# Four row buffers for the experts' gathers, beta added between scatters, and sixteen successive tokens per partition

## The reference, cut to what matters

```python
x = x + tanh(g_xattn[0]) * L0_xattn(layernorm(x), ctx)
x = x + tanh(g_ffn[0])   * L0_ffn(layernorm(x))      # shared expert + top-1 of 8, silu(gate) * up, down
x = x + tanh(g_xattn[1]) * L1_xattn(layernorm(x), ctx)
x = x + tanh(g_ffn[1])   * L1_ffn(layernorm(x))      # top-2 of 8, relu, down
# L1_ffn ends with
y = mixed + x_in                       # x_in: the layernormed rows; mixed: weighted sum of two experts
return gamma * (y - mu) * rsqrt(var + eps) + beta
```

## Time and profile before

| | |
|---|---|
| median of 3 runs | 1531.54 us (1530.1 to 1533.1) |
| the profiled execution | 1530.35 us |
| its span in the trace | 1528.6 us |
| PE busy | 1335.6 us, 87% of the span |
| ACT busy | 972.7 us, 64% |
| DVE busy | 561.1 us, 37% |
| POOL busy | 194.6 us, 13% |

### The profile page before, as it was taken

How to read it: one execution, slowest core, us unless ns; L and a number is a source line. 1 busy time by engine, 2 the same in 40 slices (tenths; PEclk the granted TensorE clock), 3 DMA queues, 4 the chain that set the end, 5 groups by cost and what they waited for, 6 DMA issues and landing times. The chain is left out here.

```text
span 1528.6 us, 31785 instructions
## 1 busy us (share of the span) xinstructions
PE 1335.6 (87%) x13156; PEld 699.0 (46%) x13156; DVE 561.1 (37%) x1257; ACT 972.7 (64%) x1146; POOL 194.6 (13%) x188
## 2 busy tenths in 40 slices
PE   6799999999999996999279999999999972799940
PEld 4433333333334555999233334334334332688840
DVE  7412142432333343333631223323323327333327
ACT  4499999999994323222159987987987930343322
POOL 2000000000001411332100000000000000644434
PEclk9899999999999997999679999999999985899975
DMA  7661001001114522111456100100101240121241
GB/s 206 158 113 30 23 23 27 18 18 28 26 29 151 179 78 87 49 49 39 103 160 111 27 18 16 42 17 16 41 17 50 87 136 27 49 63 63 66 141 55
DMA packets 76617, 100.80 MB, mean 66 GB/s; under 512 B 10074, under 2 KB 62302, under 8 KB 75704
## 3 DMA queue, kind: packets, MB, share of 16 engines
q1 hardware_dynamic: 70520, 82.47, 20.1%
q0 software_dynamic: 5952, 16.26, 3.3%
HBM read 67.99 MB, written 26.21 MB: 62 GB/s over the span
## 5 line engine op out<-in xcount | busy, mean ns | idle before, releaser
L1180 ACT ACTIVATE arena<-ps 128x1024 f32<-128x1024 f32 x556 | 557.5, 1247 | 56.4 <-PE ps L947 56.4
L947 PE MATMUL ps<-arena 99*32 99x512 bf16 x6656 | 463.9, 384 | 15.0 <-PEq L797 9.4
L947 PEld LDWEIGHTS ps<-arena 99*32 99x32 bf16 x6656 | 149.3, 95 | 408.5 <-issue 166.0
L1180 ACT ACTIVATE wqkv<-ps 128x1024 f32<-128x1024 f32 x276 | 298.2, 1248 | 22.7 <-PE ps L947 22.7
L963 PE MATMUL ps<-arena 128*32 128x512 f32 x2224 | 288.8, 594 | 0.8 <-ACT arena L1180 0.8
L1262 DVE COPY work<-ps 128x512 f32<-128x512 f32 x32 | 22.1, 691 | 404.6 <-PE ps L963 404.6
L1644 PEld LDWEIGHTS ps<-work,arena 128*128 128x128 f32 x1184 | 144.7, 195 | 6.5 <-DVE work L1723 3.5
L1644 PE MATMUL ps<-work,arena 128*128 128x128 f32 x1184 | 145.8, 279 | 2.1 <-DVE work L1723 2.1
L963 PE MATMUL ps<-wqkv,arena 128*32 128x512 f32 x1104 | 142.9, 593 | 0.0
L1822 POOL DMA_INDIRECT work<-xn_img,fetch x62 | 60.6, 977 | 630.5 <-POOLq L927 612.4
L1656 PE MATMUL ps<-arena,work 128*128 x496 | 119.3, 384 | 5.5 <-issue 5.0
(11 more groups left out here) (202 smaller groups left out, 1145.3 us busy)
## 6 DMA issues: line engine op xcount, KB each, us to landing
arena<-in_ew SPq DMA_DIRECT2D x16, 512.0 KB, 5.4
arena<-q_img SPq DMA_DIRECT2D x32, 192.0 KB
arena<-y_tok SPq DMA_DIRECT2D x12, 512.0 KB, 7.2
arena<-k_img SPq DMA_DIRECT2D x8, 624.0 KB, 12.7
q_img<-work SPq DMA_DIRECT2D x18, 256.0 KB, 2.6
k_img<-work SPq DMA_DIRECT2D x21, 208.0 KB, 2.5
arena<-q_img SPq DMA_DIRECT2D x32, 128.0 KB
work<-work SPq DMA_DIRECT2D x128, 32.0 KB, 2.0
```

Of the source, the lines that this page charges most:

```text
L947: last = nc.tensor.matmul(ps[i * VW:(i + 1) * VW, buf + j, :], k2[0:ROWS + SHIFT, h, at:at + VW], q2[0:ROWS + SHIFT, h, :], start=True, st ...
L1180: nc.scalar.activation(probs[(b * STEPS + u) % RING], ps[:, buf:buf + 2, :], ACT.Exp, scale=SCALE).then_inc(s_exp, 1)
```

## The change

Three edits, of which the third has several places:

1. `ROWBUFS` is 4: a fourth `rows_in` buffer, so that POOL gathers four tiles ahead of the one whose results it waits for.
2. In layer 1 `beta` is added in 16 instructions of 128 x 256, one behind each of the first 16 scatters, in place of four instructions of 128 x 1024 ahead of the loop.
3. Token `p*16 + t` is now `x[p, t, :]` (the view `(p t) d -> p t d`). A partition holds sixteen successive tokens, so the four tiles of a block are 4 KB in one piece of DRAM, 16 KB from those of the next partition, where they were four rows of 1 KB, 128 KB apart. That holds for the load of `x`, the stores to `xn_img`, the reads of `y_tok` and the store of the output. The lists follow it: `iota_turn` counts 1 to 16 twice, `own_row` has a second column with p + 128 for the second expert, and `places` computes `row*16 + turn - 1`. The number of tiles, their experts and all matmuls stay as they are; which tokens share a tile changes.

```diff
-ROWBUFS = 3
+ROWBUFS = 4
...
-        own_row, pad_row = sb("own_row", [P, 1]), sb("pad_row", [P, 1])
+        own_row, pad_row = sb("own_row", [P, 2]), sb("pad_row", [P, 1])
...
-            nc.gpsimd.iota(iota_turn[:, :], pattern=[[1, 2 * NT]], base=1, channel_multiplier=0,
+            nc.gpsimd.iota(iota_turn[:, :].rearrange("p (k t) -> p k t", t=NT), pattern=[[0, 2], [1, NT]], base=1,
+                           channel_multiplier=0,
...
-                        src = a["x"].rearrange("o (t p) d -> p (o t) d", p=P)
+                        src = a["x"].rearrange("o (p t) d -> p (o t) d", p=P)
...
-                    nc.vector.tensor_scalar(token_in_tile[l][:, :, NTL + 1:], in_tile[l], own_row[:, 0:1], None,
-                                            ALU.mult).then_inc(s_tok, 1)
+                    for k in range(L.top):
+                        js = slice(k * NT, (k + 1) * NT)
+                        last = nc.vector.tensor_scalar(token_in_tile[l][:, js, NTL + 1:], in_tile[l][:, js, :],
+                                                       own_row[:, k:k + 1], None, ALU.mult)
+                    last.then_inc(s_tok, 1)
...
-                        chain(nc.vector.scalar_tensor_tensor(out=code[:, 0:NTL], in0=turn, scalar=float(P),
+                        chain(nc.vector.scalar_tensor_tensor(out=code[:, 0:NTL], in0=row, scalar=float(NT),
...
-                        sp.dma_start(xn_img[l][b * QB:(b + 1) * QB, :].rearrange("(t p) d -> p t d", p=P),
+                        sp.dma_start(xn_img[l].rearrange("(p t) d -> p t d", p=P)[:, b * TB:(b + 1) * TB, :],
                                      xn[:, b * TB:(b + 1) * TB, :]).then_inc(s_img, 16)
...
                             sp.dma_start(got[k][:, b * TB:(b + 1) * TB, :],
-                                         y_tok[l][k * S + b * QB:k * S + (b + 1) * QB, :]
-                                         .rearrange("(t p) d -> p t d", p=P)).then_inc(s_back[b], 16)
+                                         y_tok[l][k * S:(k + 1) * S, :].rearrange("(p t) d -> p t d", p=P)
+                                         [:, b * TB:(b + 1) * TB, :]).then_inc(s_back[b], 16)
...
-                        to = out.rearrange("o (t p) d -> p (o t) d", p=P)
+                        to = out.rearrange("o (p t) d -> p (o t) d", p=P)
...
                     for i in range(ROWBUFS):
                         fetch_rows(i)
-                    if l == 1:
-                        pool.wait_ge(s_gb, 1)
-                        for b in range(NB):
-                            nc.gpsimd.tensor_tensor(x[:, b * TB:(b + 1) * TB, :], x[:, b * TB:(b + 1) * TB, :],
-                                                    beta.unsqueeze(1).broadcast_to([P, TB, D]), ALU.add
-                                                    ).then_inc(s_xb, 1)
                     for i in range(NTL):
                         if i + ROWBUFS < NTL:
                             fetch_rows(i + ROWBUFS)
...
                             in_=rows_out[i % 2], in_offset=None).then_inc(s_st[i % 2], 16)
+                        if l == 1 and i < NT:
+                            if i == 0:
+                                pool.wait_ge(s_gb, 1)
+                            nc.gpsimd.tensor_tensor(x[:, i, :], x[:, i, :], beta, ALU.add).then_inc(s_xb, 1)
```

More of the change, by code:

```diff
@@ L422, in consts_pool @@
                            allow_small_or_imprecise_dtypes=True)
-            nc.gpsimd.iota(iota_turn[:, :], pattern=[[1, 2 * NT]], base=1, channel_multiplier=0,
+            nc.gpsimd.iota(iota_turn[:, :].rearrange("p (k t) -> p k t", t=NT), pattern=[[0, 2], [1, NT]], base=1,
+                           channel_multiplier=0,
                            allow_small_or_imprecise_dtypes=True)
-            nc.gpsimd.iota(own_row[:, :], pattern=[[0, 1]], base=0, channel_multiplier=1,
+            nc.gpsimd.iota(own_row[:, :], pattern=[[P, 2]], base=0, channel_multiplier=1,
                            allow_small_or_imprecise_dtypes=True)
-            nc.gpsimd.iota(pad_row[:, :], pattern=[[0, 1]], base=2 * S + P, channel_multiplier=1,
+            nc.gpsimd.iota(pad_row[:, :], pattern=[[0, 1]], base=2 * S + 1, channel_multiplier=1,
                            allow_small_or_imprecise_dtypes=True)
@@ L1433, in places @@
                         turn, row = ps[:, 6, 0:NTL], ps[:, 6, NTL + 1:2 * NTL + 1]
-                        chain(nc.vector.tensor_copy(pad[:, 0:NTL], row))
-                        chain(nc.vector.scalar_tensor_tensor(out=code[:, 0:NTL], in0=turn, scalar=float(P),
+                        chain(nc.vector.tensor_copy(pad[:, 0:NTL], turn))
+                        chain(nc.vector.scalar_tensor_tensor(out=code[:, 0:NTL], in0=row, scalar=float(NT),
                                                              in1=pad[:, 0:NTL], op0=ALU.mult, op1=ALU.add))
@@ L1438, in places @@
                                                       ALU.is_equal, ALU.mult))
-                        chain(nc.vector.scalar_tensor_tensor(out=dest[:, 0:NTL], in0=code[:, 0:NTL], scalar=float(-P),
+                        chain(nc.vector.scalar_tensor_tensor(out=dest[:, 0:NTL], in0=code[:, 0:NTL], scalar=-1.0,
                                                              in1=pad[:, 0:NTL], op0=ALU.add, op1=ALU.add))
```

## The result

| | before | after |
|---|---|---|
| median of 5 runs | 1530.1 us (1527.8 to 1533.1) | 1516.75 us (1513.5 to 1519.7) |
| ratio to the kernel before, 95% interval | | 0.9907 (0.9885 to 0.9930) |
| the profiled execution, its span | 1530.35, 1528.6 | 1516.75, 1515.0 |

The change makes the kernel 14 us faster (10.7 to 17.6), against a forecast of 1515.3 us (1512.5 to 1520.5).

The account below looks back on a forecast made before the run. PE was taken to bound layer 1's experts' loop, with short gather leads lengthening its steps. 1530.35 - 15.8 (loop) - 0.5 (contiguous rows) + 0.1 (lists) = 1514.15 us, as a median 1515.3, range 1512.5 to 1520.5.

Parts of the forecast that it names:

- The fourth buffer: Layer 1's loop: each gather issued one step earlier, its lead growing by 3.73 us, from 3.19 to some 6.9.
- issue: Layer 1's loop: PE stands fourteen times before the second matmuls with no known releaser, 5.0 us, blamed on late gathers.
- the silent long steps: Layer 1's loop: steps of 4.06 us or more without a visible wait, blamed on gather leads under 4 us.
- The rival that only visible waits go: Layer 1's loop: PE's own load of the expert's number causes silent long steps; gain 6.8, time 1524.3 us; 10%.
- Beta: Additions moved into layer 1's loop take 0.75 us each, POOL's step 3.3 us, under 3.73; no loss with the longer lead.
- the 1.3 us at tile 3: Layer 1's loop: PE idle 1.31 us for tile 3's gather behind beta's four additions; moving them issues it over 8 us earlier.
- Contiguous rows: Plain DMAs of `x`, `y_tok` and output, 4.2 MB or 12 us on the path: -0.5 us, bounds -1.2 to +1.2.
- The split instruction of the lists: One DVE instruction of 0.55 us becomes two halves in layer 1: 0 to 0.5 us added, taken as 0.1.
- POOL as the bound: Rival, 16 steps of layer 1's loop: additions over 1.17 us make POOL set the pace; time 1518.5 us; 7%.
- slower gathers: Rival, layer 1's loop: rows 16 KB apart land in over 7 us, so waits stay; time 1529.5 us; 3%.
- halted DMAs: Rival, plain DMAs of `x`, `y_tok` and output: 16 KB distance cuts their rate, at a third +24 us, 1539.8; 3%.
- the loop's term: Layer 1's loop, turn of tile 2 to tile 38: 36 steps at 3.73 us, 134.3 instead of 150.1, gaining 15.8 us.

Follow-up runs that it names:

- the early load: PE's load of the expert's number for `down` placed ahead of the next tile's turn, in the kernel before with three buffers: median 1517.19 us, ratio 0.9918.

## Why the prediction was right, point by point

**The fourth buffer, and what the step is.** 15.8 us were forecast for 36 steps and 15.75 came. The choice of the steps over PE's idle time in the rows (8.8 us) was what made the size right. That "issue" and the silent long steps come from the late load is shown by the early load, which brought 3.73 us steps at leads of 3.2 us with the old buffers. The rival that only visible waits go (1524.3) was right that PE's own load of the number stood behind the silent steps, and wrong that it costs them whatever the lead: with four buffers and the load where it was, all steps went to 3.73. The leads came out shorter than the 6.9 us forecast (5.1 to 6.9 from tile 5 on), since POOL's wait for its own scatters was not in the sum; the cover was wide enough.

**Beta.** The size of an addition, 0.74 us, was estimated at 0.75, the step stayed PE's: POOL by itself needs 3.19 us for it (scatters at 1333.00 and 1336.19), where 3.3 was forecast. And the cost without cover showed up alone as forecast in kind (steps of 4.5 to 5.1 us at leads of 2.8; ratio 1.002, of which a part has another cause). One attribution was off: I gave the 1.3 us at tile 3 to this edit, but four buffers alone win them. In this change the move of beta brings nothing that its sum can show.

**Contiguous rows.** The term of -0.5 us was mis-sized, and its bound of +1.2 may have been too: alone, the edit costs 0 to 3.5 us. The rates did rise, as hoped (single slices of 400 to 422 GB/s). The Trainium skill, page "DMA: Bandwidth & Descriptors", section on the iDMA fabric, gives 408.7 GB/s for a lone stream with 4 KiB rows; the slices here lie on both sides of it (338 to 422). The loss at large power-of-two row pitches, of the section "Latency and other measured facts", didn't show at 16 KB. What I left out is that a faster read must still shorten the path. The first four reads, forecast in the chain at 7.5 to 8.3 us, are no longer there; the chain goes by the first two (4.83 us) and then by DVE:

```profile
1460.92 4.83 DMA arena<-y_tok
...
1469.93 9.63 DVE arena L1808 x8
```

Three places outside the loop:

- Ahead of layer 0's loop the first turn came 1.3 us earlier (591.99 against 593.30), and the second only 0.1 (599.56 against 599.67). The timeline of PE has the first matmuls between them, after and before: the same 32 took 6.53 us where they took 5.32.

```profile
593.19 6.53 PE L1649 MATMUL ps<-work,arena 128*128 128x128 f32 x32 [0.52 <-DVE work L1728]
...
594.51 5.32 PE L1644 MATMUL ps<-work,arena 128*128 128x128 f32 x32 [0.52 <-DVE work L1723]
```

  Windows of the kernel after, and then of the kernel before (the column before the last two is the granted clock):

```profile
595.00:597.00 2.00, 2.00 (x12) 2.00 (x11) 0.03 (x1) 0.00 (x0) 0.85 (x1) 0.50 0.39 121
597.00:599.60 2.60, 2.60 (x17) 2.60 (x17) 0.00 (x0) 0.00 (x0) 0.00 (x0) 0.64 0.02 8
```

```profile
595.00:597.00 2.00, 2.00 (x11) 2.00 (x11) 1.19 (x2) 0.00 (x0) 0.61 (x1) 0.50 0.31 100
597.00:599.60 2.60, 2.60 (x23) 2.60 (x22) 0.00 (x0) 0.00 (x0) 0.00 (x0) 0.87 0.00 0
```

  Half of 2.4 GHz was granted until 597 us in both. In both PE had stood idle for 8 us before its first turn. The kernel after starts earlier and runs for longer at 1.2 GHz. It is so in all nine profiles: where the first turn comes between 591.99 and 592.58 (six), the second follows 7.24 to 7.76 us later, where it comes at 593.30 or later (three), 6.33 to 6.45. The early start itself is not shown to be the layout's: beta alone, with the old one, has it too (592.05).
- Between layer 1's first matmuls and its first turn 1.5 us are lost (762.27 to 1305.07 before, 761.98 to 1306.32 after). In 0.75 of them it is the clock again: the first eight matmuls with `wqkv` took 4.96 us and not 4.21, at a granted clock of 0.68 from 767 to 771 us against 0.83. The split instruction of the lists has 0.12 (0.1 was forecast). The rest I didn't trace.
- Behind layer 1's loop DVE is ready 0.84 us sooner and then done 0.9 later. The run without the additions of `xn` shows that the collision is with POOL. That it belongs to the layout is not shown. From first to last the eight instructions took 9.51 to 9.61 us in three profiles with the new layout and these additions, but with the old one 7.46 (beta alone), 7.87 (before), 9.51 (early load) and 9.75 (four buffers alone).

**The sum.** -16.2 was forecast and -14.2 (10.7 to 17.6) measured. The 2 us lie outside the loop, in the parts that the sum put at nothing or at -0.5, and within the interval of the measurement. They can't be booked to the layout: four buffers alone, without it, lost as much (13.8 us in the profile, of a loop gain of 15.75). POOL as the bound, slower gathers and halted DMAs all stayed away: an addition takes 0.74 us, under the 1.17 from which it decides; the gathers' median is still 2.8 us; the DMAs were faster. What the prediction got right is the loop's term; the terms outside the loop were not met, and are small beside it.

## What to carry to other kernels

Where the same step has two lengths in a timeline, set each against the lead of the transfer that it needs: a just-in-time arrival can cost a following register load even where no wait shows, and then either one more buffer or the load placed ahead of the wait cures it. Price such a loop by its undisturbed step times the count, not by the bound engine's idle rows. And before a faster transfer is booked as gain, ask what takes it back: here a clock that rises no sooner, and an addition on POOL that holds DVE. A part of the span that a change leaves alone can differ by 2 us between two profiles; only runs of each edit alone show whose loss it is.

## What the runs showed of the hardware

DVE instructions on two SBUF inputs take 0.42 us each with POOL quiet (four in 1.67 us), and one of them up to 2.62 us beside POOL additions of 128x1024 that take 2.34 to 2.63 themselves. That would fit an instruction that stands until the addition is over, which isn't shown one by one. The view by form of the kernel after (min/median/max in ns):

```profile
L1808 DVE SCALAR_TENSOR_TENSOR arena<-arena,wts x16: 472/482/2622, 1469.9 to 1491.4; 128x256 f32<-128x256 f32 x16
```

The Trainium skill, page "GPSIMD Engine Reference", section "Specifications", says that POOL shares its SBUF interfaces with VectorE and contends with instructions of two SBUF inputs; the trace agrees, and adds the price. DVE's instructions in the loop read PSUM, with one SBUF input at most, and kept their lengths beside POOL's additions (128x512 sums 0.69 us on the average in both kernels).

On PE, one load moved ahead of a wait was worth about as much (10.6 to 14.5 us) as a fourth buffer (9.5 to 14.7), with no memory spent.
